# Cross stage of a decoder layer: the totals of the slot attention as columns, turned back on TensorE

## The reference

```python
k_proj = Pn @ Wk.T; v_proj = Pn @ Wv.T          # Pn: the normed context
for _ in range(3):
    sn = rmsnorm(slots, slot_norm_w)
    q_proj = sn @ Wq.T
    scores = einsum('bkd,bmd->bkm', q_proj, k_proj) * SCALE
    attn = softmax(scores, axis=-2)              # over the slots
    attn = attn / (sum(attn, axis=-1, keepdims=True) + EPS)   # the totals
    updates = einsum('bkm,bmd->bkd', attn, v_proj)
    slots = gru_cell(updates, slots, ...)
```

## Time and profile before

| | us |
|---|---|
| three runs | 658.53, 660.25, 680.62; median 660.25 |
| profiled execution | 658.81 |
| its span in the trace | 657.1 |
| busy in the span: PE, weight loads, DVE, ACT, POOL | 619.7, 563.7, 493.0, 326.4, 229.0 |

### The profile page before, as it was taken

How to read it: one execution, slowest core, us unless ns; L and a number is a source line. 1 busy time by engine, 2 the same in 40 slices (tenths; PEclk the granted TensorE clock), 3 DMA queues, 4 the chain that set the end, 5 groups by cost and what they waited for, 6 DMA issues and landing times.

```text
span 657.1 us, 13981 instructions
## 1 busy us (share of the span) xinstructions
PE 619.7 (94%) x5064; PEld 563.7 (86%) x5080; DVE 493.0 (75%) x1037; ACT 326.4 (50%) x734; POOL 229.0 (35%) x276
## 2 busy tenths in 40 slices
PE   8889998998989999999999999999999997999995
PEld 6767786876768889999899998999988986999995
DVE  5754676666644888879888798887998988767653
ACT  6344564645565455654557545575456634131220
POOL 9612435334254422313233131331313114262543
PEclk9899999999799999999999999999999999999998
DMA  8646556457200220000000000000000000133150
GB/s 303 194 113 182 145 159 197 130 178 207 50 18 1 99 63 1 17 17 2 0 0 16 16 0 0 0 0 0 0 1 1 1 1 1 52 113 103 62 162 32
DMA packets 31374, 43.34 MB, mean 66 GB/s; under 512 B 3072, under 2 KB 18912, under 8 KB 31328
## 3 DMA queue, kind: packets, MB, share of 16 engines
q1 hardware_dynamic: 31056, 42.47, 21.6%
q10 hardware_dynamic: 272, 0.26, 0.1%
HBM read 29.39 MB, written 13.21 MB: 65 GB/s over the span
## 4 chain that ended last, share of the span: by engine, by line
PE 53%; DVE 15%; issue 14%; DMA 5%; POOL 4%; SPq 4%; ACT 3%; another core or an unknown queue 0%; DVEq 0%; POOLq 0%; ACTq 0%
PE bank L449 23%; PE bank L2172 10%; PE bank L1984 3%; DMA k_rows<-k_hl 3%; POOL hid_hl L797 3%; PE bank L1884 2%; DMA k_op<-k_rows 2%; PE bank L1842 2%; PE bank L2001 1%; PE bank L1970 1%; PE bank L1865 1%; PE bank L1849 1%; PE bank L457 1%; DVE gate_r L1636 1%; DVE attn L1380 1%
## 5 line engine op out<-in xcount | busy, mean ns | idle before, releaser
L449 PE MATMUL bank<-slots_hl,whhT_hl 128*128 128x256 f32 x864 | 113.2, 284 | 0.0
L449 PEld LDWEIGHTS bank<-slots_hl,whhT_hl 128*128 128x128 f32 x864 | 105.6, 188 | 2.5 <-ACT gate_z L1101 1.0
L2172 PE MATMUL bank<-attn_hl,vg_hl 128*128 128x256 f32 x864 | 105.9, 281 | 0.2
L2172 PEld LDWEIGHTS bank<-attn_hl,vg_hl 128*128 128x128 f32 x864 | 101.0, 188 | 4.3 <-ACT attn_hl L811 3.9
L1290 DVE TENSOR_REDUCE neg_max<-bank 128x2 f32<-128x512 f32 (+1 forms) x96 | 65.6, 690 | 50.0 <-PE bank L1851 28.6
L867 ACT ACTIVATE pT<-bank 128x512 f32<-128x512 f32 x96 | 56.9, 598 | 52.2 <-PE bank L1865 36.2
L674 POOL TENSOR_SCALAR_AFFINE_SELECT pT<-pT 128x512 f32<-128x512 f32 x64 | 40.5, 636 | 109.0 <-ACT pT L867 108.9
L688 POOL TENSOR_TENSOR sq<-sq 128x256 f32<-128x256 f32 x24 | 18.0, 751 | 170.7 <-ACT sq L1086 130.3
L797 POOL TENSOR_TENSOR hid_hl<-hid,hid_hl 128x512 fp32r<-128x512 f32 x32 | 40.8, 1303 | 25.4 <-ACT hid_hl L811 25.4
L449 PE MATMUL bank<-values_hl,hid_hl 128*128 128x256 f32 x384 | 48.4, 282 | 0.8 <-POOL hid_hl L797 0.5
L449 PE MATMUL bank<-x2T_hl,keys_hl 128*128 128x256 f32 x384 | 48.6, 284 | 0.0
(11 more groups left out here) (216 smaller groups left out, 1302.9 us busy)
## 6 DMA issues: line engine op xcount, KB each, us to landing
gate_rows<-gate_mem SPq DMA_DIRECT2D x48, 128.0 KB, 3.1
q_rows<-q_hl SPq DMA_DIRECT2D x21, 256.0 KB
k_rows<-k_hl SPq DMA_DIRECT2D x21, 256.0 KB
q_op<-q_rows SPq DMA_DIRECT2D x28, 192.0 KB, 3.4
k_op<-k_rows SPq DMA_DIRECT2D x14, 384.0 KB, 4.5
x_in<-in_x_dram SPq DMA_DIRECT2D x8, 256.0 KB, 6.7
c_in<-in_ctx_dram SPq DMA_DIRECT2D x8, 256.0 KB, 4.8
out_dram<-y_out SPq DMA_DIRECT2D x8, 256.0 KB, 2.8
```

Of the source, the lines that this page charges most:

```text
L449: mm = pe.matmul(dst, left(a), right(b), start=first and n == 0, stop=last and n == 2, skip_group_check=True)
L2172: mm = pe.matmul(halves(b)[:, m, :], vg_hl[:, j, v_part, 3 * t + r, q:q + P], attn_hl[:, j, at_part, t, :], start=n == 2 and a + m + t == ...
```

## The change

`totals` on TensorE makes two products with one column (128 totals on the partitions, two columns) and not one of 256 columns. DVE scales and inverts these two columns. A new step `inverse_totals` on TensorE turns them back into 256 columns in bank 2, the same on each partition, by two transposes, and `weights` reads them there. DVE's `totals` moves into `gates`, ahead of the last operation, `slots`; `weights` goes ahead of `mean_square`. TensorE's `scales` moves behind the first four products of `inputs`. In units 2 to 5 the order is `r`, `totals`, `z`, turning, `hn`; in the first unit after a pair change (`u` = 0 in the code, which prepares unit 1) `r`, `z`, `totals`, `hn`, turning; at a pair change the turning stands between the first and the second block of values. On ACT `attn_hi` goes ahead of `hidden_out`, and the squares of the next context and the high halves of the experts' weights go behind both.

```diff
@@ banks
         def mid(u):
-            return [(("tt", u), 2, tt_ok, UNITS, u + 1), (("r", u), 4, r_ok, UNITS, u + 1), ...
+            return [(("tt", u), 2, tt_ok, UNITS, u + 1), (("ib", u), 2, at_ok, UNITS, u + 1), (("r", u), 4, r_ok, UNITS, u + 1), ...
@@ ACT, cross
                     slots_hi(u)
-                    if u == 3 and not last:
-                        context_squares(i, 0)
-                        context_squares(i, 1)
+                    if u == 4 and not last:
+                        context_text_hi(i, 0)
+                    if u + 1 < UNITS:
+                        attn_hi(i, u + 1)
+                    if u < 5:
+                        hidden_out(i, u + 1)
+                    if u in (2, 3) and not last:
+                        context_squares(i, u - 2)
@@ DVE
             def totals(i, u):
                 dve.wait_ge(tt_mm, due(UNITS, i, u + 1))
-                dve.tensor_scalar(tot[:, :], bank[2][:, 0:T], float(D), RMS_EPS, ALU.mult, ALU.add).then_inc(tt_ok, 1)
+                dve.tensor_scalar(tot_col[:, :], bank[2][:, 0:NT], float(D), RMS_EPS, ALU.mult, ALU.add).then_inc(tt_ok, 1)
                 dve.wait_ge(tt_ok, due(UNITS, i, u + 1))
-                dve.reciprocal(inv_tot[:, :], tot[:, :]).then_inc(it_ok, 1)
+                dve.reciprocal(inv_col[:, :], tot_col[:, :]).then_inc(it_ok, 1)
             def weights(i, u):
-                dve.wait_ge(it_ok, due(UNITS, i, u + 1))
-                dve.tensor_tensor(attn[:, j, 0, :], attn[:, j, 0, :], inv_tot[:, :], ALU.mult)
+                dve.wait_ge(ib_mm, due(UNITS, i, u + 1))
+                dve.tensor_tensor(attn[:, j, 0, :], attn[:, j, 0, :], bank[2][:, 0:T], ALU.mult)
...
@@ DVE, gates
                     dve.wait_ge(cross_chain, i * CROSS_LINKS + next_link())
+                    if u + 1 < UNITS or not last:
+                        totals(i, u + 1)
                     dve.scalar_tensor_tensor(slots[:, j, :, :], diff[:, :, :], 0.5, cand[:, :, :], ALU.mult, ALU.add).then_inc(sl_ok, 1)
@@ DVE, cross
                     if u + 1 < UNITS:
-                        totals(i, u + 1)
+                        weights(i, u + 1)
                     if u + 2 < UNITS:
                         mean_square(i, u + 2, 0)
-                    if u + 1 < UNITS:
-                        weights(i, u + 1)
...
                     context_keys_lo(i, 1)
-                    totals(i, UNITS)
+                    weights(i, UNITS)
                     context_values_lo(i, 1, 0)
-                    weights(i, UNITS)
@@ TensorE
-                pe.matmul(bank[b][:, 0:T], mean_col[:, :].to_broadcast([P, P]), tot[:, :], start=True, stop=True).then_inc(tt_mm, 1)
+                for t in range(NT):
+                    mm = pe.matmul(bank[b][:, t:t + 1], tot[:, t * P:(t + 1) * P], mean_col[:, :], start=True, stop=True)
+                mm.then_inc(tt_mm, 1)
+
+            def inverse_totals(i, u, first=False):
+                b = free_bank(i, ("ib", u), first)
+                pe.wait_ge(it_ok, due(UNITS, i, u + 1))
+                for t in range(NT):
+                    mm = pe.transpose(bank[b][:, t * P:(t + 1) * P], inv_col[:, t:t + 1].to_broadcast([P, P]), ident[:, :])
+                mm.then_inc(ib_mm, 1)
@@ TensorE, inputs
+                            if n == 0 and a == 0 and (u + 1 < UNITS or not last):
+                                scales(i, u + 1)
@@ TensorE, cross
                         scores(i, u + 1)
-                        scales(i, u + 1)
                     inputs(u)
...
                         state(i, u + 1, ("r",))
-                        totals(i, u + 1)
-                        state(i, u + 1, ("z", "hn"))
+                        if u == 0:
+                            state(i, u + 1, ("z",))
+                            totals(i, u + 1)
+                            state(i, u + 1, ("hn",))
+                            inverse_totals(i, u + 1)
+                        else:
+                            totals(i, u + 1)
+                            state(i, u + 1, ("z",))
+                            inverse_totals(i, u + 1)
+                            state(i, u + 1, ("hn",))
...
                     totals(i, UNITS)
-                    context_values(i, 1)
+                    context_values_of(i, 1, 0)
+                    inverse_totals(i, UNITS)
+                    context_values_of(i, 1, 1)
+                    context_values_of(i, 1, 2)
```

More of the change, by code:

```diff
@@ L235, in decoder_layer @@
         tot = sb("tot", [P, T], where=s2)
-        inv_tot = sb("inv_tot", [P, T], where=s2)
+        tot_col = sb("tot_col", [P, NT], where=s2)
+        inv_col = sb("inv_col", [P, NT], where=s2)
         cand = sb("cand", [P, NC, T], where=s2)
@@ L296, in decoder_layer @@
         tt_mm, tt_ok, it_ok = event("tt_mm", UNITS), event("tt_ok", UNITS), event("it_ok", UNITS)
+        ib_mm = event("ib_mm", UNITS)
         at_ok, at_hi, at_lo = event("at_ok", UNITS), event("at_hi", UNITS), event("at_lo", UNITS)
@@ L380, in mid @@
         def mid(u):
-            return [(("tt", u), 2, tt_ok, UNITS, u + 1), (("r", u), 4, r_ok, UNITS, u + 1), (("z", u), 5, zt_ok, UNITS, u + 1),
+            return [(("tt", u), 2, tt_ok, UNITS, u + 1), (("ib", u), 2, at_ok, UNITS, u + 1), (("r", u), 4, r_ok, UNITS, u + 1), (("z", u), 5, zt_ok, UNITS, u + 1),
                     (("hn", u), 6, hb_ok, UNITS, u + 1)]
@@ L394, in decoder_layer @@
             jobs2 += front(UNITS)[:1] + context(0)[1:] + context(1)[:1] if u == 4 else []
-        jobs2 += context(1)[1:2] + mid(UNITS)[:1] + context(1)[2:] + [(("uT", 0), 2, x2_ok, 2, 1)] + front(UNITS + 1)[:1]
-        jobs2 += mid(UNITS)[1:] + [(("uT", 1), 0, x2_ok, 2, 2)]
+        jobs2 += context(1)[1:2] + mid(UNITS)[:2] + context(1)[2:] + [(("uT", 0), 2, x2_ok, 2, 1)] + front(UNITS + 1)[:1]
+        jobs2 += mid(UNITS)[2:] + [(("uT", 1), 0, x2_ok, 2, 2)]
         BANK2 = {job[0]: job[1] for job in jobs2}
@@ L408, in decoder_layer @@
                       ("ss", UNITS + 1): (2, rb_ok, due(UNITS, -1, UNITS + 1)), ("tt", UNITS): (2, ms_ok, due(UNITS, -1, UNITS + 2)),
+                      ("ib", UNITS): (2, it_ok, due(UNITS, -1, UNITS + 1)),
                       ("r", UNITS): (4, a_ok, 2 * B - 1), ("z", UNITS): (5, a_ok, 2 * B), ("hn", UNITS): (6, x1T_ok, B - 1)}
@@ L1129, in cross @@
                         copy(part[:, HI, half, :], staged[:, half, :]).then_inc(ffn_hi, 1)
[L1130 to L1133, removed]
-                    if u + 1 < UNITS:
-                        attn_hi(i, u + 1)
-                    if u == 4:
-                        hidden_out(i, u + 1)
                     if u == 4 and not last:
@@ L1397, in totals @@
                 dve.wait_ge(tt_mm, due(UNITS, i, u + 1))
-                dve.tensor_scalar(tot[:, :], bank[2][:, 0:T], float(D), RMS_EPS, ALU.mult, ALU.add).then_inc(tt_ok, 1)
+                dve.tensor_scalar(tot_col[:, :], bank[2][:, 0:NT], float(D), RMS_EPS, ALU.mult, ALU.add).then_inc(tt_ok, 1)
                 dve.wait_ge(tt_ok, due(UNITS, i, u + 1))
-                dve.reciprocal(inv_tot[:, :], tot[:, :]).then_inc(it_ok, 1)
+                dve.reciprocal(inv_col[:, :], tot_col[:, :]).then_inc(it_ok, 1)
             def weights(i, u):
                 j = u % 2
-                dve.wait_ge(it_ok, due(UNITS, i, u + 1))
-                dve.tensor_tensor(attn[:, j, 0, :], attn[:, j, 0, :], inv_tot[:, :], ALU.mult)
-                dve.scalar_tensor_tensor(attn[:, j, 1, :], attn[:, j, 1, :], s_inv[:, j, 1:2], inv_tot[:, :],
+                dve.wait_ge(ib_mm, due(UNITS, i, u + 1))
+                dve.tensor_tensor(attn[:, j, 0, :], attn[:, j, 0, :], bank[2][:, 0:T], ALU.mult)
+                dve.scalar_tensor_tensor(attn[:, j, 1, :], attn[:, j, 1, :], s_inv[:, j, 1:2], bank[2][:, 0:T],
                                          ALU.mult, ALU.mult).then_inc(at_ok, 1)
@@ L2047, in first_context @@
                     context_values_of(-1, 1, 2, True)
+                    inverse_totals(-1, UNITS, True)
             def project_first(b, batch, which):
```

## The result

The changed kernel took 660.96 us (median of 22 runs, 656.22 to 667.18), the kernel before 658.46 us (22 runs beside them): a ratio of 1.0051, 95% interval 1.0028 to 1.0074. That is 0.5% slower, some 3.4 us, and within the 2% of "no change". The ratio leaves out runs over 1.5% above the fastest of their kernel; the two medians differ by 2.5 us. The profiled execution of the changed kernel took 659.8 us with a span of 658.0.

What follows compares the result with a forecast made beforehand. Two tied loops were taken to bound a unit of 11.28 us: TensorE's work and the chain through `slots`. Terms -0.4 - 0.6 - 1.4 + 4.0 + 0.3 = +1.9 gave 660.7 us, range 650 to 666.

Steps and rivals of the forecast that it cites:

- The forecast's likeliest case: Whole kernel: the summed terms hold, 660.7 us, with its own range 658 to 664; chance 0.50.
- Two tied loops: In a unit of 11.28 us, TensorE's work and the way through `slots` both bind; a change gains only by shortening both.
- rival A: TensorE's floor rules: every unit runs at 11.08, -12 us in all, 647 us; chance 0.14.
- TensorE's floor: TensorE's own work in an ordinary unit after the change: 84 products at 0.116 plus 0.45, 0.45, 0.22, 0.22, 11.08 us.
- Ordinary units: Nine units, three in each of three pairs: 11.28 - 0.62 + 0.28 + 0.30 = 11.24 us each, -0.4 in all.
- First units: First unit of four pairs: `totals` behind `z` delays `slots` by 1.6, 0.64 comes back; +1.0 each, +4.0 in all.
- rival C: First units: `gate_z` comes earlier once DVE is relieved, `z` starts at once, they stay as they are; 657 us, chance 0.20.
- Pair change: Three changes: `scales` -0.3, transpose into bank 2 waiting for `weights` +0.5, four new transposes +0.4; taken as +0.1 each, +0.3.
- most of both lies beside DVE's own row of work: At pair changes: most of the +0.5 wait for `weights` and +0.4 for transposes is hidden, leaving +0.1 each.
- Rival B: Pair change: POOL's 1.75 us operation holds the ports first, `slots` waits about 1.3 longer; +3.9, 665 us; chance 0.16.
- the prediction's reading of the 1.11: Pair change: `slots` took 1.11 us beside POOL's work, 0.69 alone, taken to agree with the exclusive lock on shared ports.
- Last pair: Three units fall from 11.85 to 11.66, -0.6; the last `inputs` starts at +10.4, not +11.85, -1.4.

## Why the prediction was right, and where its terms were off

The verdict and the size are right: +1.9 forecast, +3.4 by the ratio (+2.5 between the medians) and +3.0 by the stretches. The forecast's likeliest case is also the one that the profile shows in all stages but the pair change. That the sum came so close is in part luck: the ordinary units and the pair changes each came out 0.7 above their terms and the last pair 0.4, the first units 0.8 below.

- *Two tied loops.* Right. TensorE stayed over 99% busy and DVE lost 8.5 of 64 us, and units stayed at 11.3. That the `slots` loop came last is shown by the run with the small totals behind `slots`: the first two units of a pair fell to 11.15 and 11.02. With that rival A falls: the units stood above TensorE's floor of 11.08 because of the chain, and reached it when the chain was shortened (11.02 is 0.06 under the floor as I had put it).
- *Ordinary units.* -0.04 forecast, +0.03 measured. In the unit shown the sum is right to 0.01 (11.25 against 11.24), with two errors that cancel: `slots` to mean squares took 1.54, not 1.66, and mean squares to `inputs` 1.96, not 1.84, most of it in `scores` (340.96 to 342.45, 1.49 instead of 1.39). What I had not seen is that one unit doesn't stand for nine: of the three in a pair the first takes 11.39 to 11.46 and the third 11.31 to 11.37; the second, the one that I had worked out, is the one that gained (11.23 to 11.25).
- *First units.* Right in mechanism, each wait at its place, and rival C is refuted: DVE waits for TensorE there, and TensorE for `gate_z`, which comes hardly earlier for the room on DVE (`z` starts at 313.21 - 306.32 = +6.89, before at 314.37 - 307.37 = +7.00). The term was +1.0 each and measured +0.5, +0.8, +0.9 and +1.0.
- *Pair change.* Here the size was off: +0.1 each forecast, +0.44, +0.29 and +0.24 measured. The step that failed is "most of both lies beside DVE's own row of work". The transpose into bank 2 did wait for `weights`, 0.62 (0.5 was forecast), and this stood on the path, as the run with `weights` first showed. What hid the difference is unit 4 to 5, which lost 0.4 to 0.5, more than the 0.3 that I had given it.
- *Rival B* did not occur. The timeline of DVE and POOL after, beside the earlier trace rows:

```profile
295.21 0.83 DVE L1661 SCALAR_TENSOR_TENSOR slots<-diff,cand 128x512 f32<-128x512 f32 x1
296.08 1.67 DVE L1665 TENSOR_TENSOR slots<-slots,x1T 128x512 f32<-128x512 f32 x1
...
294.34 1.15 POOL L691 TENSOR_TENSOR sq<-sq 128x256 f32<-128x256 f32 x1 [10.97 <-ACT sq L939]
295.46 1.76 POOL L695 TENSOR_TENSOR slots_hl<-x1T,slots_hl 128x512 fp32r<-128x512 f32 x1
```

and what the earlier trace rows leave out, POOL's sum of squares before the change:

```profile
295.84 0.80 POOL L688 TENSOR_TENSOR sq<-sq 128x256 f32<-128x256 f32 x1 [9.07 <-ACT sq L936]
```

`slots` still begins 0.25 ahead of POOL's operation of 1.76 (0.52 before) and took 0.83, less than the 1.11 of before. So the prediction's reading of the 1.11 was incomplete. `slots` began 0.55 before the end of POOL's sum (296.09 to 296.64) and now begins 0.28 before it (295.21 to 295.49): the shift that I feared took it away from POOL's work ahead of it and made it shorter. What stood beside POOL's long operation was the residual behind it, before the change (1.68) as after (1.67), where 0.68 is its time alone. The rule of the Trainium skill (SBUF — State Buffer, section "SBUF: two separate sides"), by which the one that starts first keeps the other out for its whole length, agrees nearly: by it, as an estimate, the residual would end 0.68 behind POOL's 297.22, at 297.90, and it ended at 297.75.
- *Last pair.* Both terms right in sign, a little large: -0.4 against -0.6, and the last `inputs` -1.2 against -1.4.

## What to carry to other kernels

Where an engine is 99% busy, look for the second loop before counting on its busy time: if the chain through the other engines returns just when the busy engine does, relieving a third engine does not shorten the unit (8.5 us of 64 off DVE gave nothing here). That thinning the busy engine alone would not either follows from the rows, but no run here tried it. In a queue, put a small operation behind the operation that the long chain hangs on, unless another engine waits for the small one; the same two operations were worth 0.2 to 0.3 us ahead or behind in a unit, and the other way round, 0.7, at a pair change. A product that can run early belongs into the time in which the next one waits for its bank, not behind it.

## What I had not expected

Moving two transposes of 0.40 us four products back was worth 4.2 us in all, because POOL's scales were 0.29 to 0.31 late where they had stood, even with `attn_hi` early; and in the versions with late `weights`, where POOL's inverse root took 0.70 and not 1.15, the same move was worth nothing between the first and the last `inputs`. A DVE operation of 128x512 took 0.67 to 0.69 alone, and 0.83, 1.07, 1.11 or 1.67 near POOL's operations, by when it started. And a wait of 1.10 for `weights` at the head of ACT's queue came out again in the next unit, in a `soft` that does not need those `weights` at all, through a copy on ACT and the operation of DVE that waits for it.
